# Filling the first half of an attention stack from SBUF tiles instead of by way of DRAM

## The reference

```python
q = x @ Wq; k = x @ Wk; v = x @ Wv
latent_kv = (k + v) @ W_down_kv
k_rec = latent_kv @ W_up_k; v_rec = latent_kv @ W_up_v
# 16 heads of 8 columns, B = 2, S = 1024
scores = einsum('bhqd,bhkd->bhqk', qh, kh) * scale      # scale = 1 / (sqrt(128) + 1e-8)
scores = clip(nan_to_num(scores), -10000, 10000)
scores = scores * exp(-0.0001 * |i - j|)
scores = clip(nan_to_num(scores), -10000, 10000)
out = softmax(scores) @ vh ; out @ Wo
```

## Time and profile before

| | |
|---|---|
| median of 3 runs | 969.34 us (967.95 to 970.76) |
| the profiled execution, its own time | 973.44 us |
| its span, first to last instruction | 972.0 us |
| PE busy | 775.5 us (80%) |
| DVE busy | 627.5 us (65%) |
| ACT busy | 463.8 us (48%) |
| POOL busy | 218.4 us (22%) |
| mean share of full TensorE clock granted | 0.877 |

### The profile page before, as it was taken

One profiled execution on the slowest core, in us unless ns is written; L12 is line 12 of the kernel. 1 busy time (PEld: TensorE's weight loads), 2 busy tenths in 40 slices (PEclk: granted clock), 3 DMA queues, 4 the chain that ended last, 5 costly groups with the idle time before them and its releaser, 6 DMA issues. The chain is left out here.

```text
span 972.0 us, 25623 instructions
## 1 busy us (share of the span) xinstructions
PE 775.5 (80%) x10829; PEld 464.3 (48%) x10829; DVE 627.5 (65%) x1854; ACT 463.8 (48%) x682; POOL 218.4 (22%) x228
## 2 busy tenths in 40 slices
PE   6376999999999999999853876999999596026990
PEld 3001554555555555554442763666666354024670
DVE  3787878998997989891054113677767644762344
ACT  4520677777776777778821344343333322001222
POOL 3982121121212121211203644000000000005531
PEclk9555899999999999999975896999999798557995
DMA  6562213131313132000066114500000002201104
GB/s 187 145 187 89 69 31 72 27 71 35 70 36 66 38 62 44 5 3 5 3 204 194 40 40 144 182 1 2 1 1 1 0 1 66 68 1 37 40 26 141
DMA packets 45750, 59.10 MB, mean 61 GB/s; under 512 B 11925, under 2 KB 22878, under 8 KB 45633
## 3 DMA queue, kind: packets, MB, share of 16 engines
q1 hardware_dynamic: 42512, 51.47, 20.0%
q0 software_dynamic: 2304, 4.74, 1.9%
q10 hardware_dynamic: 816, 1.23, 0.4%
HBM read 42.09 MB, written 15.07 MB: 59 GB/s over the span
## 5 line engine op out<-in xcount | busy, mean ns | idle before, releaser
L819 DVE CUSTOM_DVE_ANT_0 junk<-row,rest 128x512 bf16<-128x512 f32 x448 | 294.1, 691 | 35.6 <-PE row L417 34.8
L639 ACT ACTIVATE prob<-score 128x1024 f32<-128x1024 f32 x256 | 253.0, 1026 | 86.1 <-PE score L417 85.6
L417 PE MATMUL score<-stack 75*32 75x128 bf16 (+3 forms) x3840 | 179.1, 298 | 10.0 <-ACT prob_late L643 7.2
L417 PE MATMUL row<-stack 72*32 72x512 bf16 x1792 | 178.3, 389 | 2.7 <-DVE top L819 1.5
L505 PE MATMUL out_ps<-prob,v_aug 128*32 128x256 f32 x2048 | 151.9, 381 | 0.0
L417 PEld LDWEIGHTS score<-stack 75*32 75x32 bf16 x3840 | 86.0, 97 | 79.9 <-ACT prob_late L643 16.8
L720 POOL TENSOR_SCALAR_AFFINE_SELECT prob<-prob 128x512 f32<-128x512 f32 x64 | 40.8, 637 | 272.3 <-ACT prob L639 272.3
L417 PEld LDWEIGHTS row<-stack 72*32 72x32 bf16 x1792 | 47.4, 95 | 62.5 <-DVE top L819 48.9
L505 PEld LDWEIGHTS out_ps<-prob,v_aug 128*32 128x32 f32 x2048 | 61.0, 111 | 30.1 <-issue 0.9
L1367 PE MATMUL up_ps<-rows_t,up_w 128*128 128x320 f32 (+1 forms) x192 | 62.4, 451 | 7.8 <-DVE rows_t L1579 5.0
L1886 PE MATMUL outs<-vm_w,mixed 128*64 128x256 f32 x512 | 61.7, 381 | 1.8 <-issue 1.8
(11 more groups left out here) (306 smaller groups left out, 1103.6 us busy)
## 6 DMA issues: line engine op xcount, KB each, us to landing
stack<-parts_dram SPq DMA_DIRECT2D x288, 64.0 KB
parts_dram<-prob SPq DMA_DIRECT2D x12, 256.0 KB, 6.7
parts_dram<-stack SPq DMA_DIRECT2D x12, 256.0 KB, 3.8
results<-x_tok SPq DMA_DIRECT2D x12, 256.0 KB, 3.6
up_w<-in_L_ffn_w_dram SPq DMA_DIRECT2D x1, 2048.0 KB, 10.0
rows<-x_tok SPq DMA_DIRECT2D x8, 256.0 KB, 3.1
y<-results SPq DMA_DIRECT2D x8, 256.0 KB, 4.1
up_w<-in_L_ffn_wg_dram SPq DMA_DIRECT2D x1, 2048.0 KB, 11.1
```

What stands on the lines that cost most here:

```text
L417: last = pe.matmul(out[c:c + 32, :], keys[:, c:c + 32], queries, start=True, stop=True)
L639: act.activation(prob[tile % 2][:, h, :], score[n % 2][:, :], ACT.Exp).then_inc(exped, 1)
L819: dve.tensor_tensor_reduce(junk[:, n % 2, :], row[:, n % 2, :], rest[:, at:at + HALF], 1.0, LOWEST, ALU.mult, ALU.max, top[:, 0, h, tile, ...
```

## The change

Of group 0's half 0, the 18 loads from DRAM are replaced by 72 DMAs straight from the tile of parts to the stack, one for each of the 4 heads, since a DMA's rows must be consecutive partitions on both sides. They are issued part by part, ahead of the six stores of the same parts, which stay (groups 1 to 3 still read them). The stores of half 1 now wait until the six stores of half 0 have landed. The four `reach` are moved to stand between DVE's steps for the parts of batch 0, and read one factor from the PSUM bank of the projection; PE's `values` wait for them, because they overwrite those banks. The comparison in the limits takes the missing factor SCALE0 into account.

```diff
+        def place_rows(sp, side, n):
+            sp.wait_ge(part[0][n], side + 1)
+            for m in range(NPART):
+                a, k = ((n, m), (m, n))[side]
+                at = (a * NPART + k) * HD
+                for h in range(GH):
+                    sp.dma_start(stack[0][at:at + HD, 0, side, h, :],
+                                 parts[0][0][h * HD:(h + 1) * HD, side, n, :]).then_inc(first_in, 16)
...
             order = ((0, 0), (0, 1), (0, 2), (1, 0), (1, 1), (1, 2))
             for side, k in order:
+                place_rows(sp, side, k)
+            for side, k in order:
                 store_parts(sp, 0, 0, side, k, kept[side][k])
-                if (side, k) == (0, 2):
-                    for n in range(NPART):
-                        sp.wait_ge(kept[0][n], 16)
-                        for m in range(NPART):
-                            load_rows(sp, dram, stack[0], 0, 0, 0, n, m, stacks_in[0][0])
-            for n in range(NPART):
-                sp.wait_ge(kept[1][n], 16)
-                for m in range(NPART):
-                    load_rows(sp, dram, stack[0], 0, 0, 1, m, n, stacks_in[0][0])
+            for side in range(2):
+                for k in range(NPART):
+                    sp.wait_ge(kept[side][k], 16)
             for side, k in order:
                 store_parts(sp, 0, 1, side, k, stored[0])
...
             pe.wait_ge(raw_copied[1, 0], 2)
+            pe.wait_ge(reached, 2)
             values(0, 4)
             pe.wait_ge(raw_copied[1, 1], 2)
+            pe.wait_ge(reached, 4)
             values(1, 6)
...
-                    pe.wait_ge(stacks_in[0][0], LOADS * 16)
+                    pe.wait_ge(first_in, LOADS * GH * 16)
...
-                        pe.wait_ge(stacks_in[0][g.third], (g.round + 1) * LOADS * 16)
+                        pe.wait_ge(stacks_in[0][g.third], (g.round + (g.third > 0)) * LOADS * 16)
...
             def reach(b, side):
                 dve.wait_ge(raw_copied[b, side], 2)
-                n = 2 * b + side
-                if n:
-                    dve.wait_ge(reached, n)
-                dve.tensor_tensor_reduce(junk[:, :, :].rearrange("p a t -> p (a t)"), raw[b][:, side, :], raw[b][:, side, :], 1.0, 0.0,
+                if b or side:
+                    dve.wait_ge(reached, 2 * side + b)
+                n, of = 2 * b + side, (score[side], (out_ps[:, :], row[:, :, :].rearrange("p a t -> p (a t)"))[side])[b]
+                of = of[:, :]
+                dve.tensor_tensor_reduce(junk[:, :, :].rearrange("p a t -> p (a t)"), of, raw[b][:, side, :], 1.0, 0.0,
                                          ALU.mult, ALU.max, extent[:, n:n + 1]).then_inc(reached, 1)
...
             first_left(0)
+            reach(0, 0)
             second_left(0)
+            reach(1, 0)
             scale(1)
+            reach(0, 1)
             first_left(1)
+            reach(1, 1)
             second_left(1)
-            for b in range(B):
-                for side in range(2):
-                    reach(b, side)
...
-                    dve.tensor_scalar(limits[:, 14:15], limits[:, 12:13], 0.9 * CLAMP * CLAMP, None, ALU.is_lt).then_inc(settled, 1)
+                    dve.tensor_scalar(limits[:, 14:15], limits[:, 12:13], 0.9 * CLAMP * CLAMP / float(SCALE0), None, ALU.is_lt).then_inc(settled, 1)
```

More of the change, by code:

```diff
@@ L211, in attention @@
         stacks_in = [[sem(f"stacks_in{half}_{i}") for i in range(3)] for half in range(2)]
-        lowest_in = sem("lowest_in")
+        lowest_in, first_in = sem("lowest_in"), sem("first_in")
         v_staged = sem("v_staged")
```

## The result

The changed kernel takes 999.88 us in the median of 4 runs (994.55 to 1002.09), the kernel before beside it 970.05 (967.95 to 971.82): a ratio of 1.0302, with a 95% interval of 1.0266 to 1.0337. It is slower by 3%, eight times as much as forecast and outside the range. The profiled execution has a span of 997.7 us and an own time of 999.16.

A forecast was written before the change was run, and what follows sets the result against it. PE's wait for the first stack fill was taken as the bound. Issues and landing add 3.8 us, squares, PE's waits, limits and the hidden second branch zero: 969.34 + 3.8 = 973.1, taken as 973.0; range 966 to 977.5.

The forecast's parts named there:

- What bounds the kernel now: Group 0's start: PE waits 14.2 us for the first stack fill; moving the wide rows' start moves the end one for one.
- The price of an issue: SP's queue ahead of the wide rows: 72 issues at 0.345 us each, between 0.29 and 0.41, ending at 40.85.
- The landing: Last copy into the stack: lands 2.3 us after its issue, between 2.0 and 3.7, so PE starts at 42.8.
- The cover of the squares: DVE's moved `reach` delay side 1's last part to 27.7, hidden because SP reaches it at 36.7; zero cost, otherwise 2.3 us.
- The second branch: Half 1's stores and loads, then POOL's `v_aug` before the first column unit: +8.8 us, hidden with 1.3 of 6.3 us left.
- rival B: POOL's `values_set` before the first column unit becomes the bound through longer landings: +6.7 to +8.5 us, 976 to 977.8; chance 0.13.
- Rival A: SP's issues are cheap, clearly under 0.345 us, so the saved round trip counts: 963 to 967 us; chance 0.20.
- Carrying the shift through: From the wide rows to the kernel's end: the +3.8 us start shift reaches column unit, at 97.6, and end unchanged.

The follow-up runs named there:

- e6: Changed kernel with v_aug set early and the third stack cleared only after the negated maxima are turned; ratio 1.0238 to the kernel before.
- e2: Changed kernel with the largest squares as before: after VectorE's parts, both factors from SBUF, no TensorE wait; ratio 1.0304 to the kernel before.
- e3: Kernel before with only the new order and PSUM factor of the largest squares, stack still filled through DRAM; ratio 1.0004.
- e1: Kernel before with group 0's 18 loads of half 0 split into 72 of one head each, still from DRAM; ratio 1.015.
- e5: Kernel before with 32 extra copies ahead of the output projection; 8-row issues held SyncE 0.59 to 0.64 us between SBUF tiles, 0.30 with DRAM.
- e10: Kernel before with v_aug set early and the third stack cleared after the negated maxima are turned, nothing else; ratio 0.9989.
- e11: Changed kernel with each part placed once by four copies, its other two places filled by two 64 KB stack-to-stack copies; ratio 1.0097 to the kernel before.
- e9: Kernel before with half 0's side 1 stores issued by ScalarE, one factor of the squares from PSUM, and the late memset; ratio 0.9924.
- e7: Kernel before with the three stores of side 1 of half 0 issued by ScalarE right behind its casts; ratio 0.9977.

## Why the prediction was wrong, step by step

- **What bounds the kernel now:** right. The starts of the wide rows that the experiments moved by 1 to 27 us moved the first column unit by the same within 2 us, in all but e6, where the column unit waited for SyncE.
- **The price of an issue, the step that failed.** "I take 0.345, the row with the same destination and row length", with 0.41 as the upper end. Measured: 0.677. With it the prediction's own sum gives 16.05 + 71 x 0.677 + 2.3 = 66.4, and the wide rows started at 66.22. All rows that I compared had DRAM on one side; the only copy between SBUF tiles in the trace stood in my own rows, two `neg_rows` in 1.74 us, 0.87 each. I used it to bound the landing and not the issue. I varied size and row count and never the kind of the two ends. As an upper end it would have made 16 + 62 + 2.3 = 80, and the range would have held the result.
- **The landing:** 2.3 forecast, 2.0 measured (64.2 to 66.22).
- **The cover of the squares:** right. Four of 1.22 us, the last part ready at 27.1 (27.7 forecast), hidden by SyncE: e2, with the squares where they were before, starts at the same 66.20. Without that cover they were to cost 2.3 us; e3 shows 1.8 us at the wide rows.
- **The second branch (rival B):** right in place and wrong in form. Since both branches wait for the same 72 issues, they moved together: loads from 76.02 (44.29 before), POOL's clearing from 113.94 (81.59 before), 32.4 us later against 27.2 of the wide rows. POOL was done at 119.74, and without the 3.1 us that the memset cost the cast, PE would have wanted it at 122.78 - 3.1 = 119.7: of the 6.3 us of slack nothing was left, where 1.3 had been forecast. The branch also has a second arm that the prediction left out: SyncE issues the negated rows only after its own wait for batch 1's stores (`stored[1]`), the wait that held e6's column unit.
- **Rival A:** fell. The Trainium skill's rule in "DMA: Bandwidth & Descriptors", "Issuing engines are not separate DMA queues", is that the time to initiate a DMA is usually small beside the DMA itself. The trace disagrees for these copies: one issue, 0.677 us, is a third of the 2.0 us from issue to landing, and 72 in a row keep the queue for 48.8 us, so the queue and not the data sets the end.
- **Carrying the shift through:** 29.0 us at the first column unit, 30.6 at the end of the attention, 29.8 between the medians. The granted clock of the wide rows is 0.50 in both kernels, so PE's longer idle time ahead of them took nothing there, and from the first column unit to the end of the attention both need about the same (394.2 and 395.7 us). The profiled span grew by only 25.7, as 6 us came back in the expert mixture, between the DMAs `rows<-share` and `y<-results`: 64.4 us before (516.2 to 580.6), 57.9 after (547.5 to 605.5). That is a difference between executions, or chips, and not the change's: no experiment touches this stretch, and it takes 57.4 to 58.2 us in the profiled executions of e1 to e5, e10 and e11 and 63.3 to 63.9 in those of e6 to e9, which ran on another chip.

The Trainium skill's page "SBUF — State Buffer", "SBUF: two separate sides", describes the port pair that VectorE and GpSimd share as a lock held for a whole instruction, the loser blocked until it ends; a VectorE operation takes part in it in a two-port mode, or with two SBUF inputs, and then only against a GpSimd operation that reads SBUF. The trace agrees: the cast ended with the memset, after 3.28 us, and the subtraction with two SBUF inputs, also inside the memset, took 0.19. That the cast runs in a two-port mode no run shows.

## What to carry to other kernels

Before a round trip through DRAM is replaced by direct copies, count the issues and price them by both ends of the copy, SBUF or DRAM, from a row of that very kind; the nearest row by size is not the nearest row. A round trip that is spread over few issues can be faster than many small direct copies, and small steps may be worth more than the large one: e9 moved three stores to another queue, one factor of the squares to PSUM and a memset out of the way, and gained 0.8%, where the first and the last of these steps alone (e7, e10) gave nothing that can be measured. Where GpSimd is released by a late transfer, ask what VectorE is doing at that moment: a memset moved by some microseconds can hit a short chain that it used to miss.

## What was not expected of the hardware

- An issue on SyncE of a copy from SBUF to SBUF: 0.59 to 0.64 us in the median for 1 to 128 rows of 2 KB (four each), 0.624 over the 72 of the changed kernel; with DRAM on one side 0.30 us for 8 rows, 0.43 to 0.44 for 128.
- Start of the wide rows by the count of such issues ahead of them: 66.2 with 72, 48.75 with 36 (and nine loads), 45.03 with 36 that carry the same bytes as 72.
- A VectorE cast of 128 x 32 elements took 3.28 us instead of 0.18 beside a GpSimd memset of 32 x 4096 that began 0.26 us before it; a subtraction of the same size beside the same memset took its usual 0.19.
